# Three batches' expert rows in one chain of 13 tiles, two SSM states folded on the partitions, spare products on TensorE, and another stage order

## The chip, the cores and the metric

One core of one Trainium2 chip runs the kernel. The metric is device time in microseconds (us), the median of some executions. PE is TensorE, DVE VectorE, ACT ScalarE, POOL GpSimd, and SP the engine whose queue starts most DMAs.

## What is computed

Two layers over x of 4 x 512 tokens x 256 values, all in float32; every step is added to x and reads a layer norm of it:

```python
x = x + attn0(norm(x))   # per token: 16 heads against one key, softmax, times one value
x = x + ffn0(norm(x))    # 2 experts, FF 1024, each token goes to the expert with the larger gate
x = x + ssm(norm(x))     # 256 channels x 8 states
x = x + ffn1(norm(x))    # 64 experts, 6 per token, plus a shared expert
...
# ffn0: h = silu(x @ w_gate[e].T) * (x @ w_up[e].T); y = top_w * h @ w_down[e].T
# ssm:
delta = softplus(dt_r @ W_dt.T + b_dt)
dA  = exp(delta[..., None] * A)
dBu = (delta * x)[..., None] * B_ssm[:, :, None, :]
h   = scan over l of (h * dA + dBu)
y   = einsum('bldn,bln->bld', h, C_ssm) + x * D_param
```

## The kernel before

**Order.** The work of the 4 batches is cut into stages (`name.batch.part`). One written list, `plan`, gives their order; every engine runs the stages in which it has a part, in that order, and semaphores join the engines. So an engine that waits in one stage holds back all that follows in its own part of the list, the DMA issues of SP and POOL too.

**ffn0.** The tokens of a batch (512) are sorted by expert in DRAM into 5 tiles of 128 rows (`S0`), expert 0 from the top and expert 1 from the bottom, so that every tile has one expert, whatever the split. `route_gate` and `route_slots` compute each token's row on DVE with small operations on 128x4 values (lines 1124 to 1153), one waiting for the other; POOL scatters the rows (`sorted_dram`, one for each batch), SP loads them (`ffn_load`), PE turns them (`ffn_in`). A tile has two halves of 512 of the 1024 inner columns: `ffn.b.s` makes gate and up products (L679), ACT a tanh (L902), DVE two operations (L1161, L1166); `ffn_h` turns the result (L628), and `ffn_down` makes 16 products for a tile (L696). SP stores the tiles and POOL gathers a batch's rows back (`ffn_out`), after which DVE adds them to x (L1176). `ffn_load` of batch 1 and of batch 3 waits until the rows of all batches are sorted, since its buffer covers that of the norm's output.

**ssm.** `ssm_norm` (DVE), `ssm_in` (turns), `ssm_proj` (L709, L715: B and C rows, then delta's argument), `ssm_exp` and `ssm_delta` (softplus on ACT and DVE, up to L1204). SP writes the 16 rows of B and C to DRAM and loads them again, copied to all 128 partitions, into `bc` (4096 KB; L489, L492). Right behind it in SP's queue, `ssm_exp` fills 4 x 768 KB of `part_rows` with zeros (L505), for the last stage of the kernel. Then there are 8 groups, `ssm.b.g`: one group is 2 states of one chunk of 128 channels, 128x1024 values. ACT makes `d_a` (`ssm_a`, L966), and DVE multiplies (L1217), scans (L1221) and multiplies (L1224). PE adds the group's two states into one PSUM bank with 128x128 identity products (`ssm_sum`, L728); ACT copies the sum of a chunk (`move_sum`), PE turns it back (`ssm_out`) and DVE adds it to x (L1231).

**ffn1.** `gates_in`, `gates`, `places`, `rounds` (top 6 and the list of tokens of each expert, on DVE), the shared expert (`shared_mm`, L761; `shared`; `shared_out`, L779), and behind the list 32 pairs of experts, whose gate and up products (L808) and down products (L826) fill half of PE's columns each: the two experts of a pair are written to partitions 0 to 63 and 64 to 127 of one bank.

## Time and profile before

| what | value |
|---|---|
| time, median of 3 runs | 717.83 us (717.29 to 720.01) |
| the profiled execution: its own time, its span | 719.09 us, 717.4 us |
| busy share: PE, DVE, ACT, POOL | 83%, 71%, 28%, 15% |
| mean granted PE clock | 0.91 of full |
| chain that ended last: PE, DVE, DMA, ACT | 49%, 32%, 7%, 5% |
| batch 0's rows reach x after ffn0 | 143.0 us |
| x after the ssm of batch 0, 1, 2, 3 | 237.9, 337.9, 437.7, 532.7 us |
| first pair of experts of ffn1, last one's end | 568.2, about 668 us |

The span runs from the first to the last instruction. The marks in the lower rows are starts of single instructions, in us from the start of the span. 4 x 5 tiles of ffn0 and 32 groups of the ssm lie between 63 and 520 us.

### The profile page before, as it was taken

How to read it: one execution, taken by the hardware profiler on the slowest of the kernel's cores; microseconds unless marked ns; L12 is line 12 of the kernel's file. 1: busy time of each engine (PE TensorE's matmuls, PEld its weight loads, DVE VectorE, ACT ScalarE, POOL GpSimd, SP SyncE). 2: the span in 40 equal slices, each digit the busy share in tenths (PEclk: the TensorE clock that was granted, in tenths of full speed). 3: DMA queues.
4: the chain of work that ended last, by engine and by line, in shares of the span. 5: the costliest groups of instructions: out<-in, count | busy, mean ns of one | idle time of the engine just before them, and what ended most of it. 6: DMA issues, size and time to landing. Idle time of an engine off the chain costs nothing.

```text
span 717.4 us, 7176 instructions
## 1 busy us (share of the span) xinstructions
PE 595.6 (83%) x2225; PEld 327.3 (46%) x2225; DVE 512.9 (71%) x1100; ACT 198.1 (28%) x387; POOL 104.7 (15%) x119
## 2 busy tenths in 40 slices
PE   4359998879998869998889988887656699999875
PEld 3235555525555446554355643553243244444554
DVE  7967966155995859997579998699985545555364
ACT  1112221226332334431543232521301133332000
POOL 2022021200002000002000010000000446664200
PEclk9757998998999959999899999999875899999999
DMA  7940000309202192011471010997004579998497
GB/s 276 399 147 32 1 31 15 118 2 359 89 0 67 32 375 80 0 38 30 175 236 37 1 52 16 348 352 230 0 1 164 176 249 364 363 370 294 152 415 290
DMA packets 50371, 114.35 MB, mean 159 GB/s; under 512 B 6112, under 2 KB 32992, under 8 KB 49824
## 3 DMA queue, kind: packets, MB, share of 16 engines
q1 hardware_dynamic: 42576, 94.88, 37.2%
q0 software_dynamic: 5456, 16.91, 6.9%
q10 hardware_dynamic: 2304, 2.10, 0.8%
q8 instruction: 20, 0.33, 0.2%
q14 instruction: 15, 0.12, 0.1%
HBM read 84.26 MB, written 29.62 MB: 159 GB/s over the span
## 4 chain that ended last, share of the span: by engine, by line
PE 49%; DVE 32%; DMA 7%; ACT 5%; issue 4%; SPq 2%; POOL 1%; DVEq 0%; POOLq 0%; ACTq 0%
DVE scan_area L1221 8%; PE gate_ps L808 6%; PE gate_ps L679 6%; PE up_ps L679 6%; PE misc_ps L696 5%; DVE scan_area L1224 4%; DVE scan_area L1217 4%; PE turn_ps L628 4%; DMA bc<-part_rows 3%; PE ssm_ps L728 3%; PE ssm_ps L826 3%; PE misc_ps L826 2%; DVE sig L1161 2%; PE turn_ps L651 2%; PE gate_ps L761 2%
## 5 line engine op out<-in xcount | busy, mean ns | idle before, releaser
L679 PE MATMUL gate_ps<-big,front_area 128*128 x160 | 84.5, 655 | 1.9 <-ACT front_area L866 1.9
L696 PE MATMUL misc_ps<-big,front_area 128*128 x320 | 74.6, 387 | 6.1 <-ACT front_area L866 3.4
L1221 DVE TENSOR_TENSOR_SCAN scan_area<-scan_area 128x1024 f32<-128x1024 f32 x32 | 73.3, 2292 | 7.0 <-ACT scan_area L966 3.4
L679 PE MATMUL up_ps<-big,front_area 128*128 x160 | 77.9, 610 | 0.0
L728 PE MATMUL ssm_ps<-scan_area,ident 128*128 128x512 f32 x128 | 63.3, 629 | 10.6 <-DVE scan_area L1224 9.9
L696 PEld LDWEIGHTS misc_ps<-big,front_area 128*128 128x128 f32 x320 | 61.5, 194 | 23.1 <-issue 15.3
L902 ACT ACTIVATE sig<-gate_ps 128x512 f32<-128x512 f32 (+1 forms) x52 | 30.9, 594 | 104.4 <-PE up_ps L679 67.8
L679 PEld LDWEIGHTS up_ps<-big,front_area 128*128 128x128 f32 x160 | 32.3, 202 | 42.6 <-issue 42.6
L966 ACT ACTIVATE scan_area<-scan_area,a_col 128x511 f32<-128x511 f32 x64 | 42.2, 714 | 33.2 <-DVE scan_area L1221 30.6
L1161 DVE SCALAR_TENSOR_TENSOR sig<-sig,gate_ps 128x512 f32<-128x512 f32 (+1 forms) x52 | 35.5, 682 | 21.5 <-ACT sig L902 14.2
L628 PE MATMUL turn_ps<-ident,front_area 128*128 128x128 f32 x208 | 34.1, 297 | 18.3 <-DMA g_row<-in_gate 10.1
L586 POOL DMA_INDIRECT front_area<-ysorted_dram,slot_idx x16 | 17.3, 1083 | 208.8 <-DMA ysorted_dram<-front_area 205.1
L651 PE MATMUL turn_ps<-w_qkv,front_area 128*128 128x288 f32 x64 | 27.3, 596 | 20.0 <-ACT front_area L866 13.6
L728 PEld LDWEIGHTS ssm_ps<-scan_area,ident 128*128 128x128 f32 x128 | 24.1, 195 | 42.1 <-issue 23.3
L679 PEld LDWEIGHTS gate_ps<-big,front_area 128*128 128x128 f32 x160 | 30.0, 206 | 28.1 <-issue 28.0
L628 PEld LDWEIGHTS turn_ps<-ident,front_area 128*128 128x128 f32 x208 | 26.9, 153 | 34.6 <-issue 21.1
L866 ACT COPY front_area<-turn_ps 128x512 f32<-128x512 f32 (+1 forms) x62 | 34.2, 568 | 24.1 <-PE turn_ps L628 22.7
L1224 DVE TENSOR_TENSOR scan_area<-scan_area,bc 128x1024 f32<-128x1024 f32 x32 | 39.2, 1224 | 1.1
L1217 DVE TENSOR_TENSOR scan_area<-scan_area,bc 128x1024 f32<-128x1024 f32 x32 | 39.0, 1219 | 0.5 <-PE ssm_ps L728 0.2
L611 POOL DMA_INDIRECT part_rows<-bc,att_s x32 | 31.2, 975 | 37.2 <-DVE bc L1352 36.8
L595 POOL DMA_INDIRECT bc<-table,att_s x32 | 30.9, 965 | 27.2 <-DVE att_s L1334 17.7
L1359 DVE SCALAR_TENSOR_TENSOR bc<-bc,gate_ps 128x176 f32<-128x176 f32 x32 | 10.8, 337 | 29.0 <-ACT bc L1011 16.4
(213 smaller groups left out, 887.7 us busy)
## 6 DMA issues: line engine op xcount, KB each, us to landing
bc<-bc_dram SPq DMA_DIRECT2D x4, 4096.0 KB, 13.3
part_rows<-zeros SPq DMA_DIRECT2D x16, 768.0 KB, 15.4
big<-in_wgu SPq DMA_DIRECT2D x15, 704.0 KB
front_area<-in_wgu SPq DMA_DIRECT2D x9, 704.0 KB
big<-part_rows SPq DMA_DIRECT2D x8, 768.0 KB, 10.0
scan_area<-in_wgu SPq DMA_DIRECT2D x6, 704.0 KB
big<-in_wd SPq DMA_DIRECT2D x15, 256.0 KB
front_area<-part_rows SPq DMA_DIRECT2D x5, 768.0 KB, 20.3
```

The costliest lines, as they stand in the source:

```text
L628: mm = pe.transpose(turn_ps[slot][0:width, col:col + rows], src, ident[0:rows, 0:rows])
L651: mm = pe.matmul(turn_ps[slot][:, 0:QKV], xn_attn_t[:, k, j, :], w_qkv[:, k, :], start=(k == 0), stop=(k == K - 1))
L679: mm = pe.matmul(bank[:], xs_t[:, k, j, :], gu0[:, expert_of[b, j], k, g, half * 512:(half + 1) * 512], start=(k == 0), stop=(k == K - 1))
L696: mm = pe.matmul(misc_ps[:, 0:D], h0_t[:, half, c * P:(c + 1) * P], dn0[:, expert_of[b, j], half * 4 + c, :], start=(half == 0 and c == 0) ...
L728: mm = pe.matmul(ssm_ps[:], ident[:], hs[:, g % HS_RING, n, :], start=False, stop=(g % PER_CHUNK == PER_CHUNK - 1 and n == GROUP - 1))
L808: mm = pe.matmul(gate_ps[p % 2][e * CAP:(e + 1) * CAP, 0:FSH], xg_t[:, p % 2, k, e * CAP:(e + 1) * CAP], gu1[p % RING][:, e * K + k, :], s ...
L826: mm = pe.matmul(y_ps[par][e * CAP:(e + 1) * CAP, 0:D], h1_t[0:rows, par, c, e * CAP:(e + 1) * CAP], dn1[p % RING][c][:, e * D:(e + 1) * D ...
L966: nc.scalar.activation(d_a[:, g % 2, n, 1:L], delta[:, c, 1:L], ACT.Exp, scale=a_col[:, c, n0 + n:n0 + n + 1]).then_inc(da_ready, 1)
L1161: stt(out=s, in0=s, scalar=1.0, in1=gate_ps[slot][0:rows, :], op0=ALU.add, op1=ALU.mult).then_inc(silu_steps, 1)
L1217: tt(buf, sp_z[:, c, :].unsqueeze(1).broadcast_to([P, GROUP, L]), bc[:, n0:n0 + GROUP, :], ALU.mult).then_inc(dbu_ready, 1)
L1221: nc.vector.tensor_tensor_scan(buf.rearrange(flat), d_a[:, g % 2, :, :].rearrange(flat), buf.rearrange(flat), 0.0, ALU.mult, ALU.add).then ...
L1224: tt(buf, buf, bc[:, NS + n0:NS + n0 + GROUP, :], ALU.mult).then_inc(hc_ready, 1)
```

## The change

It has four parts.

1. **Chain.** Batches 1, 2 and 3 share one sorted tensor of 13 tiles; batch 0 keeps its own of 5. `TILES_OF` is 5, 5, 4, 4, so that 18 tiles are computed instead of 20. The small operations that find a row grow: `RT_OPS` is 15, 21, 27 and 31 instead of 15 for each. `ffn_load` of batches 1, 2 and 3 all wait for the sorted rows of all batches.
2. **Two states on the partitions.** A group is now one state on partitions 0 to 63 and another on 64 to 127, for two blocks of 64 channels. The loaded B and C rows are 8 instead of 16 for a partition (2048 KB). `delta` and `delta * x` are copied to the new layout by 4 DMAs of 256 KB each (`spread`), in SP's queue behind the zeros of `ssm_exp`. PE adds the two halves with a 128x64 matrix `fold`, and each block goes to its own half of the bank's partitions.
3. **Spare products.** 39 stages `awake` of two 128x128 products of 256 columns each, on zeros: 16 in the stages of batch 0's attention, 23 behind `ssm_out.3`.
4. **Order.** Another `plan`; besides, the first turns of PE wait for no weights any more, and the first `attn_qkv` waits for the attention's matrices alone.

```diff
+TILES_OF = [S0, S0, J, J]
+TILE_AT = [sum(TILES_OF[0:b]) for b in range(B + 1)]
+CHAIN_AT = [0] + [TILE_AT[b] - S0 for b in range(1, B + 1)]
+CHAIN = (TILE_AT[B] - S0) * P
+Q = P // 2
+BLOCKS = D // Q
+SHARE = NS // 2
-RT_SEL, RT_DIFF, RT = J + 1, J + 2, J + 11
+RT_OPS = [J + 11, J + 17, J + 23, J + 27]
...
-        bc = sb("bc", [P, 2 * NS, L])
+        scan_in = sb("scan_in", [P, 2 * SHARE + 2 * BLOCKS, L])
+        bc = scan_in[:, 0:2 * SHARE, :]
+        delta_wide = scan_in[:, 2 * SHARE:2 * SHARE + BLOCKS, :]
+        du_wide = scan_in[:, 2 * SHARE + BLOCKS:, :]
...
             def ffn_load(b, _):
-                wait_apart(sp, passed["sp"], (rows_sorted, (B if b % 2 else b + 1) * 16 * J))
+                wait_apart(sp, passed["sp"], (rows_sorted, (B if b else 1) * 16 * J))
...
-                sp.dma_start(bc[:].rearrange("p n l -> p (n l)"), ...broadcast_to([P, 2 * NS * L])
+                for i in range(2):
+                    sp.dma_start(bc[i * Q:(i + 1) * Q, :, :]..., ...broadcast_to([Q, 2, SHARE * L])).then_inc(bc_loaded, 16)
+            def spread(wide, narrow, signal):
+                for h in range(2):
+                    for i in range(2):
+                        sp.dma_start(wide[i * Q:(i + 1) * Q, :, :].rearrange("p (c h) l -> p h c l", h=2)[:, h, :, :],
+                                     narrow[h * Q:(h + 1) * Q, :, :]).then_inc(signal, 16)
+            def ssm_delta(b, _):
+                wait_apart(sp, passed["sp"], (z_steps, (b + 1) * ZS))
+                spread(delta_wide, delta, delta_spread)
+                wait_apart(sp, passed["sp"], (du_ready, b + 1))
+                spread(du_wide, sp_z, du_spread)
...
+            def awake(b, _):
+                if b == 0:
+                    pe.wait_ge(pool_consts, 12)
+                else:
+                    pe.wait_ge(y_moved, B * K)
+                for _ in range(2):
+                    pe.matmul(ssm_ps[:, 0:D], ident[:], zeros[:, 0:D], start=True, stop=True)
...
             def ssm_sum(b, g):
                 for n in range(GROUP):
-                    mm = pe.matmul(ssm_ps[:], ident[:], hs[:, g % HS_RING, n, :], start=False, ...
+                    mm = pe.matmul(ssm_ps[n * Q:(n + 1) * Q, :], fold[:], hs[:, g % HS_RING, n, :], start=False, ...
...
             def ssm_a(b, g):
-                    act.wait_ge(z_steps, (b + 1) * ZS)
+                    act.wait_ge(delta_spread, (b + 1) * SPREAD)
...
             def ssm_delta(b, _):                       # DVE
                 stt(out=delta, in0=sp_z, scalar=0.0, in1=soft_t, op0=ALU.max, op1=ALU.add).then_inc(s, 1)
+                dve.wait_ge(s, done + 5)
+                tt(sp_z, delta, y_fm, ALU.mult).then_inc(du_ready, 1)
             def ssm(b, g):
                 if g == 0:
-                    dve.wait_ge(bc_loaded, (b + 1) * 16)
-                if n0 == 0:
-                    tt(sp_z[:, c, :], delta[:, c, :], y_fm[:, c, :], ALU.mult).then_inc(du_ready, 1)
+                    dve.wait_ge(bc_loaded, (b + 1) * 32)
+                    dve.wait_ge(du_spread, (b + 1) * SPREAD)
-                tt(buf, sp_z[:, c, :]..broadcast_to([P, GROUP, L]), bc[:, n0:n0 + GROUP, :], ALU.mult)
+                tt(buf, du_wide[:, c * GROUP:(c + 1) * GROUP, :], bc[:, m:m + 1, :].broadcast_to([P, GROUP, L]), ALU.mult)
...
+            def chain_rows(b):
+                s, n = route_steps, RT_AT[b] + J + 6
+                count, edge0, edge1, tiles0, tiles1 = (rt_sums[:, row, :] for row in range(5))
...
+                stt(out=rank1, in0=rt[:, 9, 0:J], scalar=before, in1=rt[:, 8, 0:J], op0=ALU.add, op1=ALU.add).then_inc(s, 1)
+                ts(col(count, b), rt[:, 8, J - 1:J], before, None, ALU.add).then_inc(s, 1)
...
+                reduce(col(edge0, b), below, AX, ALU.add).then_inc(s, 1)
...
+                for g in range(1, b):
+                    dve.wait_ge(s, n)
+                    ts(part, rank1, col(edge1, g), col(tiles0, g + 1), ALU.is_ge, ALU.mult).then_inc(s, 1)
+                    dve.wait_ge(s, n + 1)
+                    tt(row1, row1, part, ALU.add).then_inc(s, 1)
+                    n += 2
...
+                tt(slot_idx[:, b, :], row0, row1, ALU.add).then_inc(s, 1)
```

Parts of the order, before and after, that the argument below speaks of:

```
before  ffn_in.0 attn_qkv.2.1 attn_qkv.2.2 route_gate.1 attn_in.3 attn_qkv.2.3 route_slots.1 ffn.0.0
after   ffn_in.0 attn_qkv.2.2 route_gate.1 ffn.0.0 ffn.0.1 attn_qkv.2.3 route_slots.1
before  ffn_out.0 ffn_in.1 ffn.1.0 ffn.1.1 ssm_norm.0 ffn_h.1.0 ffn.1.2 ssm_in.0
after   ffn_out.0 ffn_in.1 ffn.1.0 ssm_norm.0 ffn.1.1 ffn_h.1.0 ffn.1.2 ssm_in.0
before  gates_in.0 gates.0 ffn_h.2.1 places.0 rounds.0.0 ssm_exp.1 ssm_delta.1 ffn.2.3 ssm.1.0
after   gates_in.0 ssm_exp.1 ssm_delta.1 ffn_h.2.0 ffn.2.2 gates.0 ffn_h.2.1 ffn.2.3 ... places.0 ssm.1.0
after   ssm_delta.2 ffn.3.4 ffn_h.3.3 ffn.3.5 gates.1 ... places.1 ssm.2.0 ... ssm_norm.3 ssm_in.3 rounds.1.2
after   ssm_delta.0 ffn_h.1.2 ffn.1.4 ffn_h.1.3 ffn.1.5 ssm.0.0 ... ssm_delta.3 shared_out.0.1 shared.1.0..2 places.2 ssm.3.0
after   ssm_out.3 awake x8 gates_in.3 gates.3 awake x7 places.3 shared_mm.3.0 awake x5 rounds.3.0 rounds.3.1
        shared_mm.3.1 rounds.3.2 shared.3.0 awake tables.3 shared.3.1 shared_mm.3.2 awake x2 shared.3.2
```

## Rows read from the trace of the kernel before

**Rows 1.** Busy time by stretch: us, PE, PEld, DVE, ACT, POOL busy, clock, DMA.

```profile
43.20:121.00 77.80, 66.54 (x226) 40.99 (x225) 62.16 (x192) 18.45 (x42) 12.45 (x12) 0.87 0.09 29
143.00:237.90 94.90, 88.18 (x278) 47.03 (x276) 68.75 (x87) 35.33 (x59) 3.78 (x4) 0.95 0.28 98
237.90:337.90 100.00, 87.29 (x292) 49.93 (x292) 83.76 (x148) 36.86 (x61) 5.79 (x5) 0.91 0.28 99
337.90:437.70 99.80, 89.52 (x293) 49.77 (x292) 83.59 (x148) 34.80 (x58) 4.71 (x5) 0.95 0.26 93
437.70:532.70 95.00, 74.20 (x215) 38.59 (x213) 83.11 (x150) 27.15 (x41) 1.45 (x1) 0.91 0.52 176
532.70:568.20 35.50, 18.99 (x55) 10.78 (x55) 23.70 (x83) 4.22 (x9) 3.53 (x5) 0.70 0.45 150
```

**Rows 2.** Waits of DVE from 143 to 532.7: us in total, times, longest.

```profile
DVE x_res L1176 <- DMA front_area<-ysorted_dram,slot_idx: 24.7, 3, 15.8
DVE scan_area L1195 <- ACT scan_area L945: 19.1, 3, 12.1
DVE sc_s L1244 <- PE misc_ps L747: 5.7, 1, 5.7
```

**Rows 3.** Timeline of PE, ffn0 and ssm sums: start, us, instructions merged.

```profile
172.95 1.88 PE L679 MATMUL gate_ps<-big,front_area 128*128 x4
174.67 1.88 PE L679 MATMUL up_ps<-big,front_area 128*128 x4
176.39 0.60 PE L628 MATMUL turn_ps<-ident,front_area 128*128 128x128 f32 x4
...
180.26 3.62 PE L696 MATMUL misc_ps<-big,front_area 128*128 x16
...
192.31 3.60 PE L728 MATMUL ssm_ps<-scan_area,ident 128*128 128x512 f32 x8
```

**Rows 4.** Timeline of PE in the pairs of ffn1.

```profile
568.17 2.61 PE L808 MATMUL gate_ps<-big,bc 128*64 128x352 f32 x8 [0.55 <-ACT bc L1000]
...
578.50 1.40 PE L808 MATMUL gate_ps<-big,bc 128*64 128x352 f32 x8
579.83 0.44 PE L799 MATMUL turn_ps<-ident,bc 128*128 128x128 f32 x2
...
581.58 1.40 PE L808 MATMUL gate_ps<-big,bc 128*64 128x352 f32 x8
```

**Rows 5.** Groups of DVE instructions: busy us, mean ns of one, idle before.

```profile
L1221 DVE TENSOR_TENSOR_SCAN scan_area<-scan_area 128x1024 f32<-128x1024 f32 x32 | 73.3, 2292 | 7.0 <-ACT scan_area L966 3.4 <-DVE scan_area L1217 0.5
...
L1161 DVE SCALAR_TENSOR_TENSOR sig<-sig,gate_ps 128x512 f32<-128x512 f32 (+1 forms) x52 | 35.5, 682 | 21.5 <-ACT sig L902 14.2 <-issue 6.8
...
L1224 DVE TENSOR_TENSOR scan_area<-scan_area,bc 128x1024 f32<-128x1024 f32 x32 | 39.2, 1224 | 1.1
```

**Rows 6.** Timeline, batch 3: from the projection (PE) to delta (DVE), and SP's issues.

```profile
444.11 1.92 PE L709 MATMUL misc_ps<-back_t,w_x 128*48 128x512 f32 x4 [0.67 <-ACT back_t L866]
...
461.87 1.23 DVE L1204 SCALAR_TENSOR_TENSOR scan_area<-scan_area 128x1024 f32<-128x1024 f32 x1
...
448.25 0.33 SPq L492 DMA_DIRECT2D bc<-bc_dram  x1
448.61 15.30 SPq L505 DMA_DIRECT2D part_rows<-zeros  x4
```

**Rows 7.** DMA issues by line: count, KB each, median us to landing.

```profile
bc<-bc_dram SPq DMA_DIRECT2D x4, 4096.0 KB, 13.3
part_rows<-zeros SPq DMA_DIRECT2D x16, 768.0 KB, 15.4
...
table<-xf SPq DMA_DIRECT2D x4, 640.0 KB, 3.6
```

**Rows 8.** Timeline: the last of batch 3's routing on DVE, and PE's turns for batch 1.

```profile
120.50 0.16 DVE L1149 TENSOR_TENSOR rt<-tok_local,rt 128x4 f32<-128x4 f32 x1
120.69 0.16 DVE L1151 TENSOR_TENSOR slot_idx<-rt 128x4 uint32<-128x4 f32 x1
...
134.90 1.06 PE L628 MATMUL turn_ps<-ident,front_area 128*128 128x128 f32 x8 [0.91 <-issue]
```

**Rows 9.** Timeline of PE, the gate products of batch 2 and of batch 3.

```profile
469.99 1.89 PE L747 MATMUL misc_ps<-w_g,gate_t 128*128 128x64 f32 x16
...
539.79 3.68 PE L747 MATMUL misc_ps<-w_g,gate_t 128*128 128x64 f32 x16 [0.67 <-ACT gate_t L866]
```

More of the change, by code:

```diff
@@ L68 @@
 AT_DIFF, AT = 5, 10
-RT_SEL, RT_DIFF, RT = J + 1, J + 2, J + 11
+RT_SEL, RT_DIFF = J + 1, J + 2
+RT_OPS = [J + 11, J + 17, J + 23, J + 27]
+RT_AT = [sum(RT_OPS[0:b]) for b in range(B + 1)]
 SOFT_SCALE = 1.89029794104e-5 ** 0.25
@@ L406, in build @@
         order = [(*stage, 0)[0:3] for stage in order]
[L407 removed]
+        TURNS = dict(attn_turn=2, attn_qkv=1, ffn_in=(3, 3, 2, 2), ffn_h=1, ssm_in=2, ssm_out=2, gates_in=2, places=1, tables=1)
         MISCS = dict(route_slots=1, ssm_proj=1 + K, gates=1, shared_out=1, ffn_down=1)
```

258 lines of the change are left out of this document (163 added, 95 removed).

## The prediction

> **What bounds the kernel now.** I read the busy times by stretch first, cut where a batch leaves the ssm [rows 1]. From 143 to 437.7 us PE is busy for 87 to 93% of each stretch, DVE for 72 to 84%; from 437.7 to 532.7, where ffn0 is over, PE for 78% and DVE for 87%. So neither engine is far from full. One that loses work moves the end only until the other is full, and DVE is next. The second view is what DVE waits for [rows 2]: in the four stretches it is idle 389.7 - 319.2 = 70.5 us, of which 24.7 lie before L1176 (rows coming back from ffn0), 19.1 before L1195 (ACT's exponentials, behind PE's projection) and 5.7 before the gate scores (PE). The other 21 us are short waits and the gaps between instructions, some 3.6 us in a stretch. Before 121.0 both engines work through a chain of attention and routing (PE 66.5, DVE 62.2 of 77.8), and from 532.7 to 568.2 they take turns, at a mean clock of 0.70 [rows 1]. Behind 568.2 PE is busy without a hole, at 3.08 us a pair [rows 4].
>
> **Two tiles fewer.** At 2.4 GHz a half tile of ffn0 takes 1.72 us of gate and 1.72 of up products (from start to start), a turn 0.44, a tile's down products 3.45 [rows 3]. Two tiles are 4 x 3.44 + 4 x 0.44 + 2 x 3.45 = 22.4 us of PE, and on DVE 4 x 2 x 0.68 = 5.5 us [rows 5]. They go from batches 2 and 3, so they are lost from the stretches of the ssm of batches 1 and 2.
>
> **Sums by the 128x64 matrix.** Before, a group's two states cost 1.72 us (8 instructions in 3.44) [rows 3]. The trace has no 512-column product on half the columns, but the pairs' gate products are such halves: 8 instructions of 352 columns take 1.33 us from start to start [rows 4]. At the 0.84 ns per column of rows 3 they would take 2.37 if they ran one after the other, so two halves run side by side at 0.56 of that. A group then costs 0.97 us; the bounds are 0.86 (perfect) and 1.72 (no overlap). I take 0.97: 8 x 0.75 = 6 us of PE less in each batch's ssm. The pair's cycle goes from half-column products to full turns and back [rows 4], and its 3.08 us hold no hole beyond the products themselves; so I charge nothing for that change. The Trainium skill (TensorEngine Tiling (Array Packing), Key Properties) says that a change of tiling mode drains the engine; it speaks against this part, since every `ssm_sum` stands between full products. By the rule a group would cost more than 0.97; the row shows no such price.
>
> **The new copies.** Let T be the start of L709. B and C are loaded from T + 4.1, and delta is done at 461.87 + 1.23 - 444.11 = T + 19.0 [rows 6]. The zeros stand behind the load and hold SP for 15.3 us [rows 6]; the new copies stand behind the zeros. At the load's rate (4096 KB in 13.3 us [rows 7], 308 KB/us) 2048 + 3072 KB take 16.6 us: the queue is free at T + 20.7. A copy of 1024 KB then takes 3.3 us at that rate, or 5.9 at the rate of the 640 KB store that lands in 3.6 [rows 7]. So `delta` is spread by T + 24.0 to 26.6, `delta * x` by T + 27.3 to 32.5, and the first group can start. In batches 1, 2 and 3 DVE has 8.8 us of other stages in between (two halves' silu of 1.4 each, gates, places; or shared parts and places), which lasts from T + 20.2 to T + 29: the wait is 0 to 3.5 us, I take 0. In batch 0 only two silus (2.8 us) are placed there: 4 to 9 us idle, I take 4. ACT's `d_a` needs `delta` alone, which lands first. Before, the load of 13.3 us was covered in the same way, so nothing is won by its being half as large. Behind SP's two new waits stand `ffn_load.2`, `ffn_out` and in batch 3 the weights ahead, all needed much later.
>
> **Routing.** 34 small DVE operations more, each one waiting for the last, at 0.19 us [rows 8]: 6.5 us, on the path to `ffn_in.1`, which needs all rows sorted. From the last routing operation to PE's turns it is 14.1 us (120.8 to 134.9 [rows 8]), and stays so. But DVE's 15.6 us of idle time before 121.0 [rows 1] are mostly waits for PE, and `ffn.0.0` moves before three stages and starts some 5 us earlier; the spare products keep the clock up for `route_slots.0`. With 62.2 + 6.5 busy and 8 idle instead of 15.6 the routing ends 1 us earlier, with 6 idle 3 us. I take `ffn_in.1` at 132; bounds are 129 and 138 (all 6.5 added, less 3).
>
> **To 237.9.** From `ffn_in.1` three half tiles and the norm behind them come before L709: 3 x 3.44 + 2.5 of turns + 4 of copies and a cold start = 17, so T = 149. First group at T + 27 = 176. Eight groups of 1.22 + 2.29 + 1.22 + 0.1 [rows 5] are 38.6, four silus 5.5, gaps 1, and the last sum, copy, turns and the add of 5 us: x is complete at 226 instead of 237.9. That also takes in that one silu instead of two stands before `ssm_norm.0`, and that the wait before L1176 goes: the last down products now lie before three groups (14.5 us of scans), and the way back takes 9.
>
> **Batches 1, 2 and 3.** DVE bounds them: PE's 87.3 falls to 87.3 - 3.4 - 3.5 - 0.4 - 6 = 74, its 89.5 to 72. Its own work: batch 1, 83.8 - 1.4 (9 silus in the stretch instead of 10) = 82.4; batch 2, 83.6 - 2.8 (8 instead of 10) - 3.1 (three steps of `rounds.1` that move behind `ssm_norm.3`) = 77.7; batch 3, 83.1 + 3.1 = 86.2. Idle time stays: 3.6 of gaps, 4 to 5 between norm and delta (13 us of PE and ACT, filled with two silus and the next norm; with more in batch 3), 2 at the end. So 93, 87 and 93 us instead of 100, 99.8 and 95.
>
> **The end.** From 532.7 the products of `gates.3` took 3.68 at the lower clock against 1.89 in batch 2 [rows 9]; the 15 spare stages before and behind them fit into holes of 6 us. With the turns about them I take 3 us: 32.5 instead of 35.5. The first two pairs took 2.61 for 1.40 [rows 4], 2.4 us, of which the shared part now behind `tables.3` takes back 0.9: 147.7 instead of 149.2. If the clock does not rise both terms are 0, and 8 products that run at 1.2 GHz delay `gates_in.3` by up to 3.
>
> **Sum.** 226 + 93 + 87 + 93 + 32.5 + 147.7 = 679.2 us of span, against 717.4. With the 1.7 us around the span (719.09 - 717.4) it is 680.9, and since the profiled execution lay 1.3 above the median: **680 us**, 5.3% faster.
>
> **Rivals.** (a) The copies are late in every batch: with the slow rate 5 us in batch 0 and 3.5 in each other, and up to 9 more if zeros and copies disturb each other: +16 to +25, so 696 to 705. For it: SP is held 15 us at this place already [rows 6]. Against: DVE has the other stages. (b) DVE's waits go altogether: 16 us less (7 + 5.6 + 3.4), 664 and below. For it: PE has 20% of slack. Against: norm, projection and softplus are a chain of three engines. (c) Slower than before: PE, now with holes, falls to 1.2 GHz in the middle. That it does so behind a hole is seen at 568.17, 2.61 for 1.40 [rows 4]. 73 us of work with a share f at half clock take 73 x (1 + f): from f = 0.27 PE bounds a stretch again, from 0.37 nothing is won, and at 0.55 a stretch takes 113, 740 us in all. Against: with 87% busy the mean was 0.91 [rows 1], and the holes are spread over 80% work; no spare products lie there. The Trainium skill (TensorE: Matmul & The Clock Gate, Why this matters for your kernels) warns that idle gaps between bursts bring the half clock back; the trace agrees on that much. (d) The change does not do what it says, since DVE was the bound all along: sums and tiles give only DVE's 5.5 us and the 3 of the end, and the routing takes 6.5: 716, no change.
>
> **How the numbers follow.** Forecast 0.77 (668 to 694), (a) 0.10, (b) 0.07, (c) 0.03, (d) 0.03. The range reaches from (b)'s 664 to the middle of (a), which with the sums at 1.72 (+4) is 700. A measurement of this kernel tells about 0.5% from no change, 714.2 to 721.4. Faster 0.94, same 0.03, slower 0.03.
>
> **What would show it.** Right: x complete after the ssm at about 226, 319, 406 and 499 us; 18 tiles (L696's group with 288 instructions); a group's sum in 0.97 us; DVE busy for 88% or more from batch 1 to 3, and PE below 85%; the first pair at about 532. Wrong: `ffn_in.1` behind 138; a DVE wait for `du_wide` of over 4 us in batches 1 to 3; a clock under 0.8 in these stretches; sums of 1.7 us.

## The result and the profile after

The changed kernel takes 724.0 us (median of 10 runs, 722.2 to 730.3); the kernel before, run beside it, 718.7. The ratio is 1.0099, 95% interval 1.0064 to 1.0133: 1% slower, where 680 us and 5% faster were forecast. The profiled execution has a span of 721.3 us (717.4 before) and a mean granted clock of 0.891 (0.910 before).

Busy time by stretch of the changed kernel, cut where x leaves the ssm, answers to [rows 1]; the columns are the same (PE, PEld, DVE, ACT, POOL busy, clock, DMA share, GB/s):

```profile
43.20:121.00 77.80, 67.81 (x233) 41.54 (x234) 65.69 (x222) 18.46 (x42) 11.77 (x12) 0.93 0.09 31
141.70:238.90 97.20, 81.19 (x273) 43.75 (x272) 67.46 (x86) 35.01 (x58) 5.50 (x4) 0.93 0.35 94
238.90:340.40 101.50, 79.60 (x261) 40.46 (x260) 82.22 (x146) 33.54 (x55) 6.17 (x5) 0.85 0.35 95
340.40:434.20 93.80, 76.14 (x255) 41.62 (x254) 77.54 (x133) 33.54 (x55) 6.71 (x5) 0.88 0.36 98
434.20:539.80 105.60, 77.16 (x219) 41.05 (x220) 87.13 (x161) 25.84 (x39) 0.39 (x1) 0.75 0.63 192
539.80:573.30 33.50, 31.68 (x134) 22.40 (x133) 23.24 (x82) 4.23 (x9) 4.50 (x6) 1.00 0.17 56
```

DVE's work is what was forecast (82.2, 77.5 and 87.1 us for 82.4, 77.7 and 86.2). Its idle time is not: 19.3, 16.3 and 18.5 us in batches 1 to 3, where the forecast's sums leave 10.6, 9.3 and 6.8 (93, 87 and 93 less DVE's work). PE's work is not either: 79.6 and 76.1 us instead of 74 and 72, at a clock that fell from 0.91, 0.95 and 0.91 [rows 1] to 0.85, 0.88 and 0.75. Against the forecast the span is 42.1 us too long: 12.9 up to the end of batch 0, 8.5, 6.8 and 12.6 in the periods of batches 1 to 3, 1.3 behind.

What DVE waits for in these four stretches (us in total, times, longest) answers to [rows 2]:

```profile
DVE x_res L1296 <- DMA front_area<-ysorted_dram,slot_idx: 25.4, 4, 18.7
DVE sig L1281 <- ACT sig L961: 19.3, 4, 10.3
DVE scan_area L1337 <- DMA scan_in<-scan_area: 18.9, 3, 11.7
DVE scan_area L1316 <- ACT scan_area L1004: 8.7, 1, 8.7
DVE sc_s L1364 <- PE misc_ps L806: 6.2, 1, 6.2
```

In both views the largest wait of the first row (18.7 here, 15.8 before) ends where the stretch of batch 0 begins, so it lies ahead of these stretches; inside them the rows that come back from ffn0 cost 6.7 us here and 8.9 before. The wait for the softplus fell from 19.1 to 8.7 us, but the waits for silus, which in batches 0 and 2 now stand ahead of it, grew from 5.2 (below, the kernel before) to 19.3; the wait for the gate scores did not shrink.

```profile
DVE sig L1161 <- ACT sig L902: 5.2, 5, 2.6
```

The third row is new: it is the wait for the copies. It stands before the first group of batches 0, 1 and 2; the same wait of batch 3, 3.0 us, has no releaser in the profile. Batches 1 to 3:

```profile
281.46 1.23 DVE L1337 TENSOR_TENSOR scan_area<-scan_in 128x1024 f32<-128x1024 f32 x1 [5.06 <-DMA scan_in<-scan_area]
...
381.38 1.23 DVE L1337 TENSOR_TENSOR scan_area<-scan_in 128x1024 f32<-128x1024 f32 x1 [2.13 <-DMA scan_in<-scan_area]
...
482.70 1.23 DVE L1337 TENSOR_TENSOR scan_area<-scan_in 128x1024 f32<-128x1024 f32 x1 [3.02 <-issue]
```

The longest lies in batch 0. The timeline there, with T = 151.93 (PE, SP's issues, DVE), answers to [rows 6]:

```profile
151.93 1.92 PE L768 MATMUL misc_ps<-back_t,w_x 128*48 128x512 f32 x4 [0.88 <-ACT back_t L925]
...
156.07 1.24 SPq L525 DMA_DIRECT2D scan_in<-bc_dram  x2
157.35 11.41 SPq L551 DMA_DIRECT2D part_rows<-zeros  x4
171.22 8.26 SPq L533 DMA_DIRECT2D scan_in<-scan_area  x8
...
171.22 1.23 DVE L1327 TENSOR_TENSOR scan_area<-scan_area,back_t 128x1024 f32<-128x1024 f32 x1
...
186.82 1.23 DVE L1337 TENSOR_TENSOR scan_area<-scan_in 128x1024 f32<-128x1024 f32 x1 [11.73 <-DMA scan_in<-scan_area]
```

delta is done at T + 19.3, as forecast, but the first group starts at T + 34.9 instead of T + 27. (In batches 1, 2 and 3 delta is done at T + 21.2, 22.5 and 29.0, and the first groups start at T + 36.2, 34.6 and 41.5.) SP had issued the zero fills by T + 16.8; that they were still moving when the copies came is inferred from the DMA engines' share from 170 to 175 us (1.09) and from the times to landing (count, KB each, median us), which answer to [rows 7], and is tested below:

```profile
part_rows<-zeros SPq DMA_DIRECT2D x16, 768.0 KB, 14.1
scan_in<-bc_dram SPq DMA_DIRECT2D x8, 1024.0 KB, 9.6
scan_in<-scan_area SPq DMA_DIRECT2D x32, 256.0 KB, 6.1
```

Two terms came out close to their forecast. Where three groups' sums stand together at the full clock, they run in 2.72 us from start to start, 0.91 a group (forecast 0.97, [rows 3] had 1.72):

```profile
396.92 2.79 PE L787 MATMUL ssm_ps<-scan_area,fold 128*64 128x512 f32 x12
399.64 1.98 PE L820 MATMUL gate_ps<-gate_t,w_sh 128*128 128x512 f32 x4
```

and `ffn_in.1` starts its turns at 133.2 (forecast 132):

```profile
133.24 2.48 PE L678 MATMUL turn_ps<-ident,front_area 128*128 128x128 f32 x10 [5.08 <-DMA front_area<-sorted_dram]
```

But PE stands idle before the sums for 29.8 us in all, 11 times, for DVE's last product of a group.

### The profile page after: what moved, and what is told of

The parts are those of the page before. It is cut to its first block, busy times and chain, and to the rows that moved or that the text cites. A ratio compares the mean times of both kernels' runs of the same rounds, so it can differ in the third digit from the quotient of the medians.

```text
span 721.3 us, 7311 instructions
## 1 busy us (share of the span) xinstructions
PE 589.0 (82%) x2297; PEld 329.4 (46%) x2297; DVE 513.6 (71%) x1123; ACT 191.2 (27%) x375; POOL 108.2 (15%) x120
## 4 chain that ended last, share of the span: by engine, by line
PE 40%; DVE 26%; DMA 10%; ACT 5%; issue 5%; SPq 5%; POOL 1%; DVEq 0%; POOLq 0%; ACTq 0%
PE gate_ps L867 6%; DVE scan_area L1341 5%; DMA scan_in<-part_rows 4%; PE gate_ps L738 4%; SPq L533 4%; DMA scan_in<-scan_area 3%; PE up_ps L738 3%; PE turn_ps L678 3%; DVE scan_area L1344 3%; DVE scan_area L1337 3%; PE misc_ps L755 3%; PE ssm_ps L885 3%; PE misc_ps L885 2%; PE ssm_ps L787 2%; PE gate_ps L820 2%
## 5 line engine op out<-in xcount | busy, mean ns | idle before, releaser
L738 PE MATMUL gate_ps<-big,front_area 128*128 x144 | 73.6, 636 | 1.4 <-ACT front_area L925 1.4
L738 PE MATMUL up_ps<-big,front_area 128*128 x144 | 68.9, 601 | 0.0
L787 PE MATMUL ssm_ps<-scan_area,fold 128*64 128x512 f32 x128 | 38.7, 709 | 30.6 <-DVE scan_area L1344 29.8
L1025 ACT ACTIVATE scan_area<-scan_in,a_col 128x511 f32<-128x511 f32 x64 | 42.0, 715 | 54.4 <-DVE scan_area L1341 42.8
L1337 DVE TENSOR_TENSOR scan_area<-scan_in 128x1024 f32<-128x1024 f32 x32 | 39.1, 1221 | 23.5 <-DMA scan_in<-scan_area 18.9
L697 PE MATMUL ssm_ps<-zeros,ident 128*128 128x256 f32 x156 | 40.7, 417 | 9.8 <-ACT front_area L925 6.7
L697 PEld LDWEIGHTS ssm_ps<-zeros,ident 128*128 128x128 f32 x156 | 32.7, 212 | 16.8 <-ACT front_area L925 7.0
L1344 DVE TENSOR_TENSOR scan_area<-scan_area,scan_in 128x1024 f32<-128x1024 f32 x32 | 39.2, 1225 | 1.1
L738 PEld LDWEIGHTS gate_ps<-big,front_area 128*128 128x128 f32 x144 | 27.0, 206 | 24.7 <-issue 24.3
L661 POOL DMA_INDIRECT part_rows<-scan_in,att_s x32 | 31.2, 974 | 37.8 <-DVE scan_in L1472 37.0
L645 POOL DMA_INDIRECT scan_in<-table,att_s x32 | 30.9, 965 | 26.6 <-DVE att_s L1454 17.2
## 6 DMA issues: line engine op xcount, KB each, us to landing
part_rows<-zeros SPq DMA_DIRECT2D x16, 768.0 KB, 14.1
big<-in_wgu SPq DMA_DIRECT2D x15, 704.0 KB
front_area<-in_wgu SPq DMA_DIRECT2D x9, 704.0 KB
scan_area<-in_wgu SPq DMA_DIRECT2D x6, 704.0 KB
```

Of the source, the lines that this page charges most:

```text
L697: pe.matmul(ssm_ps[:, 0:D], ident[:], zeros[:, 0:D], start=True, stop=True)
L738: mm = pe.matmul(bank[:], xs_t[:, k, j, :], gu0[:, expert_of[b, j], k, g, half * 512:(half + 1) * 512], start=(k == 0), stop=(k == K - 1))
L787: mm = pe.matmul(ssm_ps[n * Q:(n + 1) * Q, :], fold[:], hs[:, g % HS_RING, n, :], start=False, stop=(g % PER_CHUNK == PER_CHUNK - 1))
L1025: nc.scalar.activation(d_a[:, g % 2, n, 1:L], delta_wide[:, c * GROUP + n, 1:L], ACT.Exp, scale=a_col[:, c * GROUP + n, m:m + 1]).then_inc ...
L1337: tt(buf, du_wide[:, c * GROUP:(c + 1) * GROUP, :], bc[:, m:m + 1, :].broadcast_to([P, GROUP, L]), ALU.mult).then_inc(dbu_ready, 1)
L1344: tt(buf, buf, bc[:, SHARE + m:SHARE + m + 1, :].broadcast_to([P, GROUP, L]), ALU.mult).then_inc(hc_ready, 1)
```

## The experiments

Each ratio is to the kernel before, timed beside it (its median lay between 717.2 and 720.2 us, so small differences between two rows are better read from the ratios). A time is a median, "x out" are the ends of the ssm of batches 0 to 3 in the profiled execution (start of the first of the two additions to x, us), "pairs" is the time from the first pair's product to the end there, and all but `no_awake` and the two chain kernels have the spare products.

| kernel | us | ratio to before | x out | pairs |
|---|---|---|---|---|
| changed kernel | 724.0 | 1.0099 (1.0064 to 1.0133) | 237, 339, 433, 538 | 148.0 |
| chain_only | 713.5 | 0.9931 (0.9895 to 0.9966) | 237, 331, 427, 522 | 148.4 |
| chain_spread | 754.9 | 1.0502 (1.0464 to 1.0540) | 249, 353, 460, 567 | 148.9 |
| no_awake | 723.2 | 1.0050 (1.0027 to 1.0073) | 238, 339, 433, 538 | 145.5 |
| no_spread | 705.5 | 0.9828 (0.9792 to 0.9864) | 230, 323, 420, 522 | 146.2 |
| zeros_late | 715.9 | 0.9943 (0.9914 to 0.9972) | 234, 331, 426, 531 | 148.0 |
| x_early | 724.4 | 1.0055 (1.0031 to 1.0079) | 238, 340, 436, 539 | 149.6 |
| full_sums | 728.4 | 1.0138 (1.0104 to 1.0172) | 237, 337, 436, 541 | 149.6 |
| best_spread | 712.8 | 0.9908 (0.9890 to 0.9925) | 232, 328, 424, 527 | 149.6 |
| delta_first | 710.5 | 0.9919 (0.9892 to 0.9946) | 230, 323, 420, 526 | 146.0 |
| warm_middle | 723.2 | 1.0092 (1.0055 to 1.0128) | 236, 339, 434, 539 | 146.7 |
| warm_fit | 717.9 | 1.0009 (0.9983 to 1.0035) | 238, 338, 433, 535 | 145.2 |
| hybrid | 700.4 | 0.9750 (0.9712 to 0.9787) | 231, 324, 419, 518 | 146.0 |
| after_fills_front | 716.5 | 0.9987 (0.9959 to 1.0016) | 235, 330, 424, 529 | 147.9 |
| fills_front | 713.8 | 0.9921 (0.9894 to 0.9948) | 232, 328, 424, 527 | 149.5 |
| hybrid_fills_front | 704.0 | 0.9808 (0.9768 to 0.9847) | 230, 324, 419, 517 | 148.0 |
| hybrid_spread | 710.4 | 0.9886 (0.9851 to 0.9921) | 230, 327, 422, 524 | 148.0 |

The last column matters, since no edit here changes the code of the pairs, yet they take 145.2 to 149.6 us. Near their start PE stands for some 2.3 us in one kernel and not in the other, and the profile names no releaser (changed kernel, then `warm_fit`):

```profile
579.94 1.40 PE L867 MATMUL gate_ps<-big,scan_in 128*64 128x352 f32 x8 [2.26 <-issue]
...
575.33 1.40 PE L869 MATMUL gate_ps<-big,scan_in 128*64 128x352 f32 x8 [0.29 <-issue]
```

Of the kernels with the new order or the mixed one, `no_awake`, `no_spread`, `delta_first`, `warm_middle`, `warm_fit` and `hybrid` lack this wait, and their pairs take 145.2 to 146.7 us; the others have it and take 147.9 to 149.6. What brings it was not found. Differences of 2 to 4 us between a kernel of one kind and one of the other are therefore no measure of what the edit did in the ssm.

### The parts of the change, one by one

`chain_only` is the changed kernel with the scan as before, no `awake` stages, and the old order less the ten ffn stages of the two tiles. `chain_spread` is the changed code in that same order. `no_awake` and `no_spread` each take one part out of the changed kernel:

```diff
# no_spread (and chain_only): what takes the place of the copies, the wide operands and the half sums
-                for i in range(2):
-                    sp.dma_start(bc[i * Q:(i + 1) * Q, :, :]..., bc_dram...broadcast_to([Q, 2, SHARE * L]))
+                sp.dma_start(bc[:].rearrange("p n l -> p (n l)"), bc_dram...broadcast_to([P, 2 * NS * L]))
-            def ssm_delta(b, _):                       # SP: both spreads
...
-                    mm = pe.matmul(ssm_ps[n * Q:(n + 1) * Q, :], fold[:], hs[:, g % HS_RING, n, :], ...
+                    mm = pe.matmul(ssm_ps[:], ident[:], hs[:, g % HS_RING, n, :], ...
```

> The chain of 13 tiles alone: the stage order of before without the ten ffn stages of the two missing tiles, both states of a group on 128 partitions as before, no spare products. Prediction's own logic (PE is relieved of 22.4 us in the ssm stretches of batches 1 and 2, DVE of 5.5, routing costs up to 6.5): about 8 us faster than before, 0.989. Theory A (the late copies ate the gain of the change) says the same, 0.985 to 0.99, since there are no copies here. Theory B (the new order and PE's holes with the lower clock ate it) says 0.985 to 0.99 too, but shows a clock in the ssm stretches of batches 1 and 2 below that of before by 0.03 or more. Theory C (DVE and the chain norm, projection, softplus were the bound all along) says no change, 1.00.

> The chain and the two states on the partitions, with all copies, in the stage order of before (without the ten ffn stages), no spare products. Against the kernel with the chain alone this gives the price of the second part by itself: fewer product columns against copies that land after delta. Theory A: the copies are as late as in the changed kernel (first group 35 us after the first projection) and cost 5 to 10 us in each batch, 20 to 40 us in all: 1.02 or more. Theory B: the copies cost little (waits of 18 us that cover other waits), the old order keeps PE warm in front of the projections: 0.98 to 0.99.

> The changed kernel without its 39 stages of spare products, all else the same. By the changed kernel's trace they bring 2 to 3 us at the end (gates at 2.00 us instead of 3.68) and perhaps 1 to 2 in front: without them 2 to 5 us slower than the changed kernel, ratio to before 1.013 to 1.017. If the spare products in front delay the attention instead, 1.005 to 1.01.

> The changed kernel (chain, new order, spare products) with the scan as before: 16 rows of B and C on all partitions, no copies of delta and delta*x, sums with the 128x128 unit matrix. Theory A: all of the loss is the copies' lateness, so the first group starts some 7 us earlier in every batch: 0.97 to 0.98. Theory B: the order made its own holes in front of the projections of batches 1 and 3, the copies only fill them: 0.995 to 1.005, with the lower clock still there.

Measured 0.993, 1.050, 1.005 and 0.983. The chain alone is faster by 0.7%, less than the 1.1% expected of it. The second part costs in both orders: 41 us in the old one (754.9 less 713.5), where the first groups start 11, 11, 14 and 12 us later behind T than in `chain_only`, and 18.5 in the new one (724.0 less 705.5; 1.8 of it lies in the pairs), where they start 11, 9, 0 and 4 us later behind T than in `no_spread`. These are net prices, what the half sums save being already in them. Without the part the change is 1.7% faster than before. The spare products do nothing for the whole that these runs tell (0.8 us between the medians, and the intervals overlap), against the 2 to 5 us that were expected of them. In the profiles they do what they are for: the clock from x of batch 3 to the first pair is 1.00 with them and 0.70 without, and the first pair starts at 573.3 instead of 577.0; but then the pairs take 148.0 us instead of 145.5. That theory A names the right part is shown; its number for `no_spread` (0.97 to 0.98) was a little too good, since here too batches 2 and 3 take longer than forecast. The same rows of `no_spread`, batches 0 to 3:

```profile
141.00:230.70 89.70, 81.58 (x267) 45.93 (x266) 66.94 (x85) 34.56 (x57) 5.30 (x4) 0.96 0.29 102
230.70:324.20 93.50, 81.40 (x267) 44.53 (x266) 82.77 (x147) 34.17 (x56) 4.82 (x5) 0.95 0.29 103
324.20:420.50 96.30, 81.42 (x257) 45.08 (x255) 77.20 (x133) 33.47 (x55) 7.31 (x5) 0.93 0.27 95
420.50:522.70 102.20, 78.38 (x213) 42.92 (x214) 86.88 (x162) 25.86 (x39) 0.40 (x1) 0.82 0.55 190
```

Its PE is busy for little longer than the changed kernel's (81.6, 81.4, 81.4, 78.4 for 81.2, 79.6, 76.1, 77.2), though its sums take 64.7 us and the changed kernel's 38.7. Of these 26 us only 9 show in PE's total; in every batch the changed kernel's clock is the lower one.

### What makes the copies late

```diff
# zeros_late: the loop of four zero fills moves from SP's ssm_exp to the end of SP's ssm_delta
                 spread(du_wide, sp_z, du_spread)
+                for j in range(J):
+                    sp.dma_start(part_of[b * J + j]..., zeros...).then_inc(parts_clear, 16)
# x_early: x is spread ahead of delta, the product is made wide, in place
             def ssm_proj(b, _):                        # SP, behind the load of B and C
+                spread(du_wide, y_fm, du_spread)
             def ssm(b, g):                             # DVE
+                if m == 0:
+                    du = du_wide[:, c * GROUP:(c + 1) * GROUP, :]
+                    tt(du, du, delta_wide[:, c * GROUP:(c + 1) * GROUP, :], ALU.mult)
# full_sums: fold stands beside 64 columns of zeros, left for n = 0, right for n = 1
+                    mm = pe.matmul(ssm_ps[:], (before_me, ones)[n][:], hs[:, g % HS_RING, n, :], ...
# best_spread: x_early and zeros_late, and delta in 8 copies of 128 KB, chunk 0 first, a semaphore for each chunk
```

> The changed kernel with SP's four zero fills of 768 KB each batch issued behind the copies of delta and delta*x instead of ahead of them. SP had issued them by T+17 (T is the start of the first product of the projection), before delta is done, but they land some 14 us after their issue, so they can still be moving when the copies start. Theory Z (the fills hold the copies up in the DMA queues): the copies land in 5 to 6 us instead of up to 11.5, first group at T+30 instead of T+35, 10 to 16 us less in all, ratio to before 0.985 to 0.995. Theory R (the copies' own issues and rate of some 205 to 270 GB/s set it): no change, 1.005 to 1.01.

> The changed kernel with x (the turned rows) copied to the wide layout right behind B and C, long before delta is done, and the product delta*x made on the wide layout after the copies of delta: half of the late copies (4 of 8 issues, 1 of 2 MB) are off the path, DVE does 2 x 1.2 us instead of 1.1 for the product. Theory R (issues of 1.03 us each and the rate of the copies behind delta): first group at T+30 to T+31 instead of T+35 in batch 0, some 3 us in each other batch, ratio to before 0.993 to 1.0. Theory Z (the zero fills ahead of them are what is waited for): first group still behind T+33, since the fills and the early copies stand ahead of delta's: 1.005 to 1.015.

> The changed kernel with the sums of a group as two products of all 128 columns (the 128x64 matrix beside 64 columns of zeros, once left and once right), so that the part saves PE nothing and only its copies remain. Theory of the prediction (half-column products side by side save PE 6 us a batch, and PE's work counts behind the first group): the time from the first group to x complete grows by 4 us a batch, as in the kernel without the copies, so +12 to +18 us, ratio 1.026 to 1.035. Theory H (PE has holes there, and fewer busy columns only bring the lower clock): 1.005 to 1.012, with a mean clock above that of the changed kernel.

> The changed kernel with all three mends of the copies: x copied early, the zero fills behind, and delta copied chunk by chunk (the first four groups need chunk 0 alone: 4 issues of 128 KB), so the first group waits for 512 KB instead of 2048. If the copies' lateness is the whole loss of this part: first group at T+25 to T+27, which gives back 16 to 22 us: ratio 0.975 to 0.985, at or below the kernel without this part (0.983). If something else of the part costs (clock, DMA reads against the scans), 0.99 or more.

`zeros_late` wins 1.6% (8.1 us between the medians): theory Z holds. Its first group of batch 0 starts at 183.7, T + 31.6, and a copy lands in 4.8 us:

```profile
171.43 7.97 SPq L533 DMA_DIRECT2D scan_in<-scan_area  x8
179.44 5.73 SPq L542 DMA_DIRECT2D part_rows<-zeros  x4
```

`x_early`, half the copies taken off the path but the fills left ahead, wins nothing by its median (724.4) and 0.4% by its ratio: theory Z again, and the first group is at T + 36.4. `full_sums` costs only 4.4 us more by its median and 2.8 by its ratio (the intervals overlap), where the prediction's logic asked for 12 to 18. PE's sums are busy for 71.9 us there instead of 38.7 and its wait for DVE in front of them falls from 29.8 to 17.1, so over a third of the saved time had turned into waiting; the mean clock is 0.909 instead of 0.891. The ratio lies between the two expectations, nearer to theory H; the half sums work, and are worth 3 to 4 us at best. With all three mends (`best_spread`) the first group is at T + 24.9 and the loss is 7.3 us against no copies at all, of which 3.4 us lie in the pairs (149.6 for 146.2); the kernel is faster than before, but the expected 0.975 to 0.985 is missed, so lateness was not the whole loss.

### Clock and order

```diff
# delta_first: no_spread, order only
-  ssm_exp.2 ffn.3.3 ffn_down.3.0 ffn_h.3.2 ssm_delta.2 ... ssm_exp.3 gates.2 shared_out.0.0 ssm_delta.3
+  ssm_exp.2 ssm_delta.2 ffn.3.3 ffn_down.3.0 ffn_h.3.2 ... ssm_exp.3 ssm_delta.3 gates.2 shared_out.0.0
# warm_middle and warm_fit: the changed kernel, awake waits for y_moved of b * K, and
-  ssm_in.1 ssm_proj.1 ... ssm_in.3 ssm_proj.3 ... gates.2
+  awake x3 ssm_in.1 awake ssm_proj.1 ... awake x13 ssm_in.3 awake ssm_proj.3 ... awake gates.2      (warm_middle)
+  awake ssm_in.1 ssm_proj.1 ... awake x7 ssm_in.3 ssm_proj.3 ... awake gates.2                       (warm_fit)
# hybrid: no_spread, new order to ssm_out.2, order of before from there to ssm_out.3
+  ssm_out.2 shared_mm.0.1 shared_mm.0.2 ssm_norm.3 ssm_in.3 rounds.1.2 ssm_proj.3 gates_in.2 shared.0.1 shared.0.2
+  shared_out.0.0 ssm_exp.3 ssm_delta.3 ... ssm.3.0 ... gates.2 ssm.3.1 ... places.2 ssm.3.3 ... ssm_out.3
```

> The kernel without the copies (chain, new order, spare products) with two stages moved: ssm_delta.2 directly behind ssm_exp.2 (ahead of ffn.3.3, for whose silu DVE stands idle 8.9 us at 345.8), and ssm_delta.3 directly behind ssm_exp.3 (ahead of gates.2 and shared_out.0.0, for which DVE is idle 4.7 and 4.0 us). Theory O (the new order puts work that waits for PE ahead of the softplus of batches 2 and 3; delta ends 23 and 26 us behind the first projection product instead of 16 and 18): delta 5 to 8 us earlier in each, and some 5 to 12 us less in all, ratio to before 0.967 to 0.976. Theory P (the stages moved back are waited for just as long where they stand now, DVE's work is the sum): unchanged, 0.98 to 0.985.

> The changed kernel with 19 more stages of spare products (2 of 256 columns each) where PE waits in front of the projections: 3 ahead of the turns of batch 1, 13 ahead of those of batch 3 (a hole of 7.6 us), 1 behind each of them, 1 ahead of gates.2. If the lower clock in these stretches (0.50 to 0.55 from 244 to 259 and from 424 to 459 us) is what costs: the x projection takes 1.9 us instead of 3.65 and the two dt products 1.1 instead of 2.07 each, so 3.6 us less in each of the two batches, and up to 2 more behind them: 6 to 10 us less, ratio 0.996 to 1.002. If it is hidden behind the copies or DVE's own chain: as the changed kernel, 1.006 to 1.012.

> The changed kernel with spare products that fit the holes: 1 stage ahead of the turns of batch 1 (a hole of 1.7 us), 7 ahead of those of batch 3 (7.6 us), 1 ahead of gates.2; a stage takes 0.93 us. The run with 19 stages had brought the projections back to 1.92 us, but its 13 stages (12.1 us) in the hole of batch 3 made the first projection product start about 6 us later, and the times cancelled. If the lower clock is a part of the loss, both batches now win what they gained from that product on (1.5 us in batch 1, 3.8 in batch 3) without the delay: 4 to 6 us less than the changed kernel, ratio 0.999 to 1.004. If it is not: 1.006 to 1.012.

> The kernel without the copies (chain of 13 tiles, spare products, states on 128 partitions as before) in the new order up to ssm_out.2 and in the order of before from there to ssm_out.3: shared_mm.0.1 and shared_mm.0.2 keep PE busy while DVE does the norm of batch 3, gates.2 and places.2 stand behind the first groups, rounds.1.2 stays behind ssm_in.3. By the marks, the new order takes 102.2 us for the ssm of batch 3 against 95.0 in the kernel with the chain alone in the old order, and the new order is 7 us better in batch 0 and 3 in the end. If these add: 4 to 7 us below the kernel without copies (0.983), ratio 0.972 to 0.978. If rounds.1.2 and the two products moved cost as much at their new places: 0.98 to 0.985.

`delta_first` missed both expectations, theory O's by most: delta came 4 and 8 us earlier (T + 19.6 in both batches instead of T + 23.8 and 27.4), the first group of batch 2 at the same time to 0.1 us (365.1), that of batch 3 4.6 us later, since the gates, places and shared parts that stand ahead of it were still to do; the kernel is slower by 5 us (0.992 to 0.983).

The clock counts. In batch 3 of the changed kernel PE waits 3.3 us for DVE ahead of the last sums; from 424 to 431 us, the time of these, its mean granted clock is 0.60, and the 8 turns at 429 already take 1.97 us for 1.04. Then PE is idle for 7.6 us ahead of the next turns, and from there to 459 us its granted clock is 0.50, the level of 1.2 GHz. So the clock had fallen before the long hole, and in the hole it stayed down:

```profile
429.08 1.97 PE L678 MATMUL turn_ps<-ident,back_t 128*128 128x128 f32 x8 [0.69 <-ACT back_t L1030]
438.62 1.94 PE L678 MATMUL turn_ps<-ident,scan_area 128*128 128x128 f32 x8 [7.58 <-DVE scan_area L1127]
441.24 3.65 PE L768 MATMUL misc_ps<-back_t,w_x 128*48 128x512 f32 x4 [0.68 <-ACT back_t L925]
445.55 2.07 PE L774 MATMUL misc_ps<-x_dbl,w_dt 32*128 32x512 f32 x2 [0.67 <-ACT x_dbl L987]
```

In batch 1 the clock is 1.00 from 235 to 243 us and 0.50 from 246 to 256, and a gap of 1.7 us precedes the fall; the projection's first product takes 3.65 us there too.

In `warm_fit` seven spare stages fill that hole and the same products run at 2.4 GHz:

```profile
431.60 6.91 PE L699 MATMUL ssm_ps<-zeros,ident 128*128 128x256 f32 x28
...
441.27 1.92 PE L770 MATMUL misc_ps<-back_t,w_x 128*48 128x512 f32 x4 [0.68 <-ACT back_t L927]
443.86 1.12 PE L776 MATMUL misc_ps<-x_dbl,w_dt 32*128 32x512 f32 x2 [0.67 <-ACT x_dbl L989]
```

and the kernel takes 717.9 us, 6 less than the changed kernel, as expected (4 to 6). But in the profiled executions, which differ by 5.4 us, only 2.6 of them are won by the first pair (570.7 for 573.3); the other 2.8 lie in the pairs, which nothing in this edit touches, so that the 6 us met the expectation partly by luck. `warm_middle` won nothing, and its 13 stages took 12.1 us in the same hole, so that the first projection product started at 447.0 instead of 441.2; for a hole of 7.6 us a stage would have had to cost 0.58 us, and it costs 0.93.

`hybrid` is the fastest of all kernels here, 0.975. Its batch 3 takes 98.1 us instead of 102.2 (the rows of `no_spread` above), and the first group of batch 3 starts at T + 25.5 instead of T + 37.2; the end up to the first pair is as long as in `no_spread`, 34.8 us from the cut:

```profile
420.10:518.20 98.10, 78.34 (x224) 42.87 (x223) 86.08 (x160) 27.14 (x41) 1.45 (x1) 0.88 0.58 201
518.20:553.00 34.80, 32.99 (x140) 23.56 (x139) 24.39 (x85) 4.23 (x9) 4.50 (x6) 1.00 0.22 72
```

### Does the second part pay with nothing beside it?

In the last four, all 16 fills are issued behind `ffn_load.0`, from some 70 us on, where the DMA engines are nearly idle (0.09 [rows 1]): in the changed kernel, with the mends of the copies (x early, delta in chunks), in `hybrid`, and in `hybrid` with the mended copies.

```diff
             def ffn_load(b, _):                        # SP
+                if b == 0:
+                    for i in range(TILES):
+                        sp.dma_start(part_of[i]..., zeros...).then_inc(parts_clear, 16)
```

> The changed kernel with all 16 zero fills (12.6 MB) issued behind the first load of sorted rows, in the stretch from some 70 to 120 us where the DMA engines are busy for 1 to 10%, instead of 4 in each batch's projection. Theory Z (the fills beside the copies are the larger part of the copies' lateness): first group at T+31 or T+32 in batch 0, as with the fills behind the copies, and the next batch's loads are free of them too: 8 to 10 us less than the changed kernel, ratio 0.990 to 0.996. If the sorting of rows (indirect DMAs from 60 to 130 us) is held up by the fills, ffn_in.1 comes later than 133 and part of it is lost: 0.997 to 1.005.

> The three mends of the copies (x early, delta in chunks) with the fills in the attention stretch instead of behind the copies. If part of the 7 us that the mended copies still cost is the fills that now run behind them and hold up the next transfers or the scans' reads: 3 us or more below the kernel with the fills behind (0.991): 0.983 to 0.987. If what is left is the second product of DVE (1.1 us a batch) and first groups that are 2 to 4 us later than without copies: 0.989 to 0.993.

> The kernel without copies in the mixed order (0.975) with the fills in the attention stretch. There the load of B and C stands ahead of the fills and nothing else waits for DMAs, so no change is expected: 0.972 to 0.978. If the fills hold up anything in the projection: up to 3 us less, 0.968 to 0.972.

> The mixed order with the second part in its mended form (x early, delta in chunks) and the fills in the attention stretch: against the run beside it, the second part's price or gain with nothing beside it. Theory L (its only cost was lateness, its gain is PE's 6 us a batch where PE is waited for): equal or up to 4 us better, 0.967 to 0.976. Theory D (DVE sets the pace behind the first group, so PE's saving stays a wait, and the first group is still 2 to 4 us later): 3 to 8 us worse, 0.979 to 0.986. The old order in batch 3 made the unmended copies cost more (41 us against 18), so more than 8 us is possible there.

`after_fills_front` gives back 1.1% (7.5 us), about as much as `zeros_late` (the intervals overlap), so it is the fills beside the copies and not the place in the queue. At 0.9987 it lies in the second range that was expected, and `ffn_in.1` does start its turns 1.3 us later, at 134.6. `fills_front` equals `best_spread`: the fills are no part of what the mended copies still cost. `hybrid_fills_front` is 3.6 us slower than `hybrid` by its median, against its expectation; 2 us of that lie in the pairs at the end (148.0 us for 146.0), where PE has the wait of 2.2 us shown above. `hybrid_spread` is 6.4 us slower than the run beside it, as theory D said, and its pairs take the same 148.0, so the 6.4 lie ahead of them: by the marks it starts its first groups 1, 2, 4 and 6 us later (176.5, 267.1, 369.5, 458.0 for 175.5, 265.4, 365.8, 452.0). So the part does not pay in the best form tried. By ratio it lies at 0.989, above theory D's range, since the run beside it is slower than expected too. Of what its mended form costs, DVE's second product (1.1 us a batch) and these later starts are seen; how much each one weighs was not measured by itself.

## Why the prediction was wrong

**The step that failed first: "the new copies".** "The queue is free at T + 20.7" took 3072 KB of fills and 2048 KB of B and C at 308 KB/us. That is the rate of a load that reads DRAM and writes SBUF; the fills, beside the load, landed 14.1 us after their issue (median), the last of them issued at about T + 14, so they were still moving behind T + 20.7. "The wait is 0 to 3.5 us, I take 0" and "in batch 0 ... I take 4" became 5.1, 2.1 and 3.0 in batches 1 to 3 and 11.7 in batch 0. (By its own rows the slow copy takes 5.8 us, not 5.9; nothing hangs on it.) 5.1 is more than the 4 us that the prediction had named as a sign of being wrong. Moving the fills alone gives back 7.5 and 8.1 us. Rival (a) had this mechanism ("zeros and copies disturb each other") at +16 to +25 us; runs with and without the part give 18.5 net, some two fifths of it the fills. What rival (a) did not have is the second step, so its 696 to 705 was too low as well. The forecast had also put delta at T + 19 in every batch; in batch 3 it is done at T + 29.0, behind gates and a shared part that each wait for PE, and there the first group is late for that reason more than for the copies.

**The step that failed next: "DVE bounds them", and "idle time stays".** DVE is busy for 81 to 83% in batches 1 to 3 and PE for 73 to 81%: neither is full, and neither alone is the bound. With the copies away (`no_spread`) the span is still 24.5 us above the forecast of 679.2: 4.7 in batch 0, 0.5 in batch 1, 9.3 in batch 2, 9.2 in batch 3, 0.8 behind. DVE's work was right, and so was its idle time in batch 1 (10.7 us). In batches 2 and 3 it is 19.1 and 15.3. The larger part of this miss is in the forecast's own sum: before, DVE was idle for 16.2, 16.2 and 11.9 us in these stretches (100.0, 99.8 and 95.0 less its work [rows 1]), and the words "stays" stood beside 10.6, 9.3 and 6.8. That is 7 and 5 us taken off batches 2 and 3 without a reason. Only some 3 us in each are idle time that was not there before, and they fit with the new order, which puts silus, gates and shared parts, each behind PE, ahead of the first group: one silu alone is waited for 8.9 us. I counted instructions per stretch and put a fixed idle time beside them; I never walked the new order stage by stage to see for which engine each one waits. `hybrid`, which changes the order of batch 3 alone, wins back some 4 us in the stretch of batch 3. `delta_first` shows that moving delta alone is no remedy, and the 9 us of batch 2 no run has won back: how they divide into the order and other causes is argued from its waits, not shown. In batch 0 the first group starts at 174.9, ahead of the forecast's 176, and 5.8 us are lost behind it. "The wait before L1176 goes" was wrong there: the rows come back 2.6 us too late in `no_spread`, 3.9 in the changed kernel. The other 3 us were not traced.

A reading failed as well. "It is idle 70.5 us, of which 24.7 lie before L1176" counts the 15.8 us that end at 143.0, where the stretch begins; 8.9 of the 70.5 are this wait, and some 37 us, not 21, were left to "short waits and the gaps", among them 7.5 us before L1311 (the shared part) and 5.2 before silus. So half of the idle time had no term of its own.

**Rival (c), given 0.03, was a real term.** PE relieved by 22 us of tiles and 26 of sums had its holes in front of the projections, and the projections of batches 1 and 3 ran at 1.2 GHz. I had argued that "the holes are spread over 80% work". They are not: DVE's norm comes at one place in every batch. A clock under 0.8 was named as a sign of being wrong, and batch 3 has 0.75. Filling these holes wins 2.6 us up to the first pair and 6 in all, of which the share in the pairs is not shown to be the clock's (`warm_fit`); rival (c) had 60 us for half the work of every stretch at half clock; with PE's busy time 5.6 and 4.1 us above the forecast in batches 1 and 2 the lower clock is a term, not the bound. The rule of the Trainium skill (TensorE: Matmul & The Clock Gate, Why this matters for your kernels) that was weighed there, that idle gaps between bursts bring the half clock back, agrees with these rows, as far as they go: in batch 1 the fall follows a gap of 1.7 us, in batch 3 gaps of 3.3 and 7.6, and the projection's first product takes 3.65 us for 1.92.

**Right:** the tiles as PE work, the sums (0.91 for 0.97), delta at T + 19 in batch 0, the end up to the first pair (33.5 for 32.5; 3.7 us later without the spare products). **Right by luck:** `ffn_in.1` at 133.2 for 132. The routing was to end 1 to 3 us earlier than before and ended 0.8 later (121.6 us); the way from there to PE's turns, which was to stay 14.1 us, took 11.6, since before PE had come to the turns straight from its own down products and now it waits for the rows. Also by luck the pairs, 148.0 for 147.7: the first ones run at 1.40 us as forecast, but the number holds only with a wait of 2.3 us that nobody forecast. The rule of the Trainium skill that was weighed there (TensorEngine Tiling (Array Packing), Key Properties), that a change of tiling mode drains the engine, shows no price here: 12 half-column products between full ones take 2.72 us, where 512 columns each, two side by side, at 0.84 ns per column are 2.6. What was saved on PE did not become time: two tiles are worth 5 us with the longer routing in it (`chain_only`), and 26 us of sums 3 to 4 (`full_sums`). Rival (d) had said that both give little; its reason, DVE as the bound, does not fit the idle time of DVE.

## What to carry to other kernels

Before counting on a copy that lies between two steps of a chain, list every transfer that was issued before it and is not yet landed, not only what stands in the issuing queue; here 3 MB of fills a batch that are read only at the end cost 8 us. Work taken from an engine at 90% becomes holes as soon as its neighbour waits elsewhere, and on PE a hole also slows what follows; so ask of each stretch where the hole will lie and what runs behind it. When a sum says that idle time stays, put the idle time of the rows into it. And where a new order comes with a change, walk it to the first place where each engine waits, and time the parts alone before the whole.
